# Two attention layers on one core: the weighted values in two blocks of four key tiles a half, instead of three blocks of three, two and three

## What is computed

```
xn  = group_norm(x, 32 groups) * gamma + beta
qkv = w_qkv @ xn + b_qkv                      # 8 heads of 32 channels
m   = softmax((q * s)^T (k * s))              # 1024 x 1024 for each head
a   = m v
x   = x + w_proj @ a + b_proj
```

## Time and profile before

| | us |
|---|---|
| three executions | 2036.97, 2041.02, 2039.26 (median 2039.26) |
| the profiled execution: its own time | 2038.87 |
| its span, first to last instruction | 2037.1 |
| PE busy | 2015.1 (99%) |
| DVE, ACT, POOL busy | 1676.5 (82%), 1242.8 (61%), 1836.8 (90%) |
| mean granted TensorE clock | 0.997 of full speed |

### The profile page before, as it was taken

How to read it: one execution, slowest core, us unless ns; L and a number is a source line. 1 busy time by engine, 2 the same in 40 slices (tenths; PEclk the granted TensorE clock), 3 DMA queues, 4 the chain that set the end, 5 groups by cost and what they waited for, 6 DMA issues and landing times.

```text
span 2037.1 us, 30395 instructions
## 1 busy us (share of the span) xinstructions
PE 2015.1 (99%) x10134; PEld 1141.0 (56%) x10134; DVE 1676.5 (82%) x2871; ACT 1242.8 (61%) x2321; POOL 1836.8 (90%) x626
## 2 busy tenths in 40 slices
PE   8999999999999999999999999999999999999998
PEld 5565555655556565555555556555565655555543
DVE  5888888888888888888888888888888888888881
ACT  2656656666665666656566566666656566565664
POOL 2799999999999999999999999999999999999984
PEclk9999999999999999999999999999999999999999
DMA  4455445644536545456554456445465454554521
GB/s 131 84 109 119 95 110 110 144 100 94 120 84 145 117 102 110 92 122 145 112 112 100 110 113 139 106 89 119 89 146 113 103 112 91 123 125 87 116 48 42
DMA packets 217307, 220.31 MB, mean 108 GB/s; under 512 B 167489, under 2 KB 167617, under 8 KB 209345
## 3 DMA queue, kind: packets, MB, share of 16 engines
q1 hardware_dynamic: 208032, 153.50, 33.6%
q0 software_dynamic: 8784, 63.97, 15.7%
q10 hardware_dynamic: 336, 0.92, 0.2%
HBM read 36.32 MB, written 16.78 MB: 26 GB/s over the span
## 4 chain that ended last, share of the span: by engine, by line
PE 94%; DVE 3%; ACT 3%; DMA 0%; issue 0%; SPq 0%; POOL 0%; DVEq 0%; ACTq 0%; POOLq 0%
PE ps_s L434 24%; PE ps_v L488 22%; PE ps_s L464 21%; PE ps_d L519 10%; PE ps_d L534 5%; PE ps_d L527 5%; PE ps_s L510 4%; ACT pt L743 2%; DVE raw_max L827 1%; ACT stage_kh L762 1%; DVE neg_max L848 1%; PE ps_s L644 0%; PE ps_s L519 0%; DMA par<-pars_dram 0%; PE ps_s L659 0%
## 5 line engine op out<-in xcount | busy, mean ns | idle before, releaser
L743 ACT ACTIVATE pt<-ps_s 128x512 f32<-128x512 f32 x2048 | 1116.7, 601 | 739.8 <-PE ps_s L434 733.1
L827 DVE TENSOR_REDUCE raw_max<-ps_s 128x1 f32<-128x512 f32 x2008 | 1289.7, 684 | 259.0 <-PE ps_s L464 254.8
L1015 POOL TENSOR_TENSOR acc<-acc,pt 128x2048 f32<-128x2048 f32 x315 | 1441.2, 4575 | 44.6 <-ACT pt L743 1.3
L464 PE MATMUL ps_s<-ks,qs 96*128 96x512 f32 x2008 | 968.6, 482 | 1.8 <-DVE neg_max L848 1.0
L434 PE MATMUL ps_s<-qs,ks 97*128 97x512 f32 x2048 | 837.2, 410 | 4.6 <-ACT pt L743 1.2
L434 PEld LDWEIGHTS ps_s<-qs,ks 97*128 97x128 f32 x2048 | 388.8, 190 | 324.8 <-issue 187.9
L464 PEld LDWEIGHTS ps_s<-ks,qs 96*128 96x128 f32 x2008 | 380.0, 189 | 182.7 <-DVE raw_max L827 75.1
L488 PE MATMUL ps_v<-pt,v 128*32 128x512 f32 x4096 | 478.7, 596 | 0.0
L1015 POOL TENSOR_TENSOR acc<-pt 128x2048 f32<-128x2048 f32 x64 | 299.6, 4681 | 58.7 <-ACT pt L743 57.1
L488 PEld LDWEIGHTS ps_v<-pt,v 128*32 128x32 f32 x4096 | 120.0, 110 | 272.6 <-issue 217.5
L519 PE MATMUL ps_d<-xn,wq 128*128 128x512 f32 x492 | 253.6, 596 | 0.0
(11 more groups left out here) (61 smaller groups left out, 601.9 us busy)
## 6 DMA issues: line engine op xcount, KB each, us to landing
acc<-pt POOLq DMA_DIRECT2D x61, 1024.0 KB, 8.5
qs<-stage_qh SPq DMA_DIRECT2D x256, 128.0 KB, 2.4
ks<-stage_kh SPq DMA_DIRECT2D x251, 128.0 KB, 2.4
qs<-stage_ql SPq DMA_DIRECT2D x128, 128.0 KB, 2.5
qs<-neg_max SPq DMA_DIRECT2D x1024, 0.5 KB, 2.1
ks<-stage_kl SPq DMA_DIRECT2D x126, 128.0 KB, 2.4
xn<-x_dram SPq DMA_DIRECT2D x16, 512.0 KB, 4.5
res<-x_dram SPq DMA_DIRECT2D x16, 512.0 KB, 4.3
```

What stands on the lines that cost most here:

```text
L464: pe.matmul(ps_m[place % RING][:, :], qs[b][0:KROWS, h, c:c + P], ks[b][0:KROWS, h, kf * HALF:(kf + 1) * HALF], start=True, stop=True).the ...
L743: act.activation(tile_of(half, t)[:, h, :], ps_t[(UNITS * s.n + u) % RING][:, :], ACT.Exp, scale=SCALE).then_inc(exp_done, 1)
L827: dve.tensor_reduce(raw_max[:, e % 2, t, kf:kf + 1], ps_m[MAX_PLACE["max", UNITS * n + w] % RING][:, :], AX.X, ALU.max)\
L1015: pool.tensor_tensor(acc[hf][:, :, :], a[:, :, :], tile_of(half, t)[:, :, :], ALU.add).then_inc(pool_added, 1)
```

## The change

The lists of units are replaced; no function changes. The order of PE's instructions changes, and with it that of the few instructions of ACT and DVE that follow a unit.

```diff
-PV_BLOCKS = {2: (-3, -2, -1), 12: (0, 1), 22: (2, 3, 4)}
-LAST_TILES = 3
-VALUES_OUT_AT = 3
-DENSE_AT = ((5, 10), (16, 20), (25, 26), (30, 33), (37, 40), (47, 51), (56, 58), (63, 64))
-SUMS_AT = 22
-SUMS_AT_END = 12
+PV_BLOCKS = {4: (-4, -3, -2, -1), 20: (0, 1, 2, 3)}
+LAST_TILES = 4
+VALUES_OUT_AT = 5
+DENSE_AT = ((7, 10), (14, 18), (23, 26), (30, 33), (40, 42), (47, 49), (54, 57), (62, 64))
+SUMS_AT = 20
+SUMS_AT_END = 4
 ROWS_AT = 7
 START_PARTS = (0, 2, 1, 3)
 V_AT, QK_AT = (1, 3, 5, 7), (1, 3)
 V_OUT_AFTER, LOW_AFTER = (3, 5), (7, 11, 15, 19)
 BUSY = 3, 12
-STATS_AT = (36, 43, 52, 53)
-GN_AT = 6
+STATS_AT = (35, 37, 51, 52)
+GN_AT = 7
```

## The result

The changed kernel takes **2048.0 us** (median of six runs, 2043.4 to 2050.1); the kernel before took 2038.0 us beside it. The ratio is 1.0048 (95% interval 1.0038 to 1.0058): slower by 10 us. The profiled execution took 2048.54 us, 9.7 more than the one of before, and its span is 2046.7.

What follows compares the result with a forecast made beforehand. PE, busy 99% of the span, was taken as the bound. Eight pairs +10.7, six pairs -1.0, four other slots -1.6, start +1 and end +2.5 gave +11.6 on 2038.87: 2050.5 us, range 2023 to 2058.

Steps and rivals of the forecast that it cites:

- the wait for half A's DMA: PE waits at unit 52's sums for POOL's accumulating DMA: 2.4 us in eight pairs, 0.7 in six.
- The runs of four: Four units without dense work, beginning with ACT's copy of q or k; a second per slot costs 0.26 us more.
- DVE and the rest of the stretches: DVE keeps up over 15 to 16 units between blocks: costed at nothing, otherwise 0.1 to 0.3 us a half.
- Fewer blocks: Four blocks a slot on PE instead of six, 0.33 us each: 1.32 us less a pair, about 21 over 32 slots.
- rival 4: Block cost grows with its tiles, so nothing is saved: near 2060 us; chance 0.02.
- Statistics later, sums earlier: Group statistics, then half A's adds and DMA, come 1.33 us later, its sums 2.46 earlier: margin shrinks by 3.79 us.
- Rival 1: The DMA's landing doesn't hold half A's sums: 2028.7 us, without the extra runs 2020.4; chance 0.24.
- rival 2: The landing holds half A's sums, but takes 7.5 us everywhere: 2038.5 us; chance 0.18.
- that rule's sum: With 2.0 us fixed DMA cost, layer 0 lands 1.3 us earlier, layer 1 0.7 later: total some 6 us lower.
- rival 3: DVE or ACT stalls PE late between longer blocks, 0.1 to 0.3 us a half: 2056 to 2064; chance 0.06.
- Half B, start: Half B's sums wait 0.2 us a pair in layer 1, 0 in layer 0; slots 0 and 1 add 1 us.
- The end: Second last half's sums move from unit 44 to 36, where PE waits for POOL's adds: +2.5 us (1 to 6).

Runs made afterwards that it cites:

- experiment 5: Changed kernel with four blocks of two tiles a half instead of two of four, two tiles left at the end: 2068.7 us.
- experiment 3: Changed kernel with POOL's scale and shift behind half A's first add and ACT's normalising instructions at units 21, 25, 29, 33: 2040.4 us.
- experiment 9: Kernel before with ACT's copy of q or k put ahead of the exponential of the same unit: 2031.3 us.
- experiment 8: Kernel before with its dense step at (37, 40) moved to (36, 38), making a run of six units without dense work: 2071.8 us.
- experiments 1 and 2: Dense steps respaced: changed kernel, (40, 42) to (39, 43) and (54, 57) to (54, 58), 2073.8 us; kernel before, (56, 58) to (56, 59), 2053.2 us.
- experiment 6: Changed kernel with only SUMS_AT_END put back from 4 to 12: 2048.9 us.

## Why the prediction was right, and where it was not

The direction and the total (2050.5 against 2048.0) came out, and each step of the path is in the trace: the statistics, the issue, the landing, the sums that wait for it. The division of the loss did not. The forecast gave the wait for half A's DMA 8 x 2.4 + 6 x 0.7 = 23 us and said that most of the gain turns into it; it was about 5, of the 31 us that stand against the gain of 21. The runs of four, put at 5 us, took 13 to 14, and DVE and the rest of the stretches, put at nothing, took 6. That these errors nearly cancel is luck: with the wait as it came and the rest as forecast, the sum would have been about 2032.

- **Fewer blocks: right.** A block of four tiles takes 3.57 us, and the score matmul behind it 0.43. 0.33 a block holds for two, three and four tiles (experiment 5), so rival 4 falls. The Trainium skill, page TensorEngine Tiling (Array Packing), section Key Properties, says "Changing tiling mode (not just tile) drains the TensorE". The trace agrees: the column tiled matmuls of line 488 pay 0.33 us once a block and nothing more per tile; that this time is the drain, no run separates.
- **Statistics later, sums earlier: right as a path.** The statistics came 10.75 us behind unit 0 against 10.5 to 10.7, the issue 31.1 to 31.4 behind that; and all 14 sums of half A begin 0.13 to 0.14 us behind the landing, where before they had 0.9 to 3.2 us to spare. Rival 1, that the landing doesn't hold the sums, falls. One size was off: PE was ready for these sums 1.7 to 1.85 us earlier in the pair than before, not 2.46, since the new run of four lies ahead of them (0.4) and the stretches there are longer (0.3).
- **The size of that wait: wrong in layer 0.** The step was "*Between landings of 7.5 and 9.7 us I take each layer's own*". Layer 0's landings took 7.4 to 8.3 us in the changed kernel, not 8.8 to 9.7, and layer 1's 7.4 to 7.6 as before. So the wait was 0.57 us in the mean of the eight pairs and 0.33 in that of the six, 0.44 and 0.20 without the 0.13 of every start, where I had 2.4 and 0.7. That was rival 2's condition, that the landings shorten, and it got a chance of 0.18. Its time of 2038.5 didn't come, because the runs and the rest cost more. A pair in layer 0 took 124.3 us, not 125. The DMA traffic in 40 slices of 0.25 us from 215 us, around layer 0's first landing, is to be laid beside the earlier trace rows:

```profile
GB/s 0 33 2 0 0 2 0 2 1 524 0 426 98 0 524 0 328 197 0 525 0 361 164 0 525 0 262 262 0 3 1 0 68 0 0 2 0 0 0 0
```

  The bulk starts at 217.25, 1.5 us behind the issue at 215.76, and ends at 222.0; the landing, 7.8 us behind the issue, is at 223.6. So traffic takes about as long as before (4.75 us), and it is the tail behind it that fell from 3.3 to 1.6 us. In layer 1 it is 1.2 (before: 1.3). The Trainium skill, page DMA: Bandwidth & Descriptors, section Anatomy of one DMA - SWDGE (gpsimd) path, has a nearly constant 2.0 us of fixed cost; the trace doesn't agree with a constant, but that rule's sum, some 6 us lower, erred by less than my rows did in this term. Why the tail shortened stays open. It isn't the later issue: in experiment 3 the issue is at 40.5 us of the pair as before, and layer 0 still lands at 7.5 to 8.8. It goes with the kernel's lists of units, blocks or dense steps: with those of before and another order on ACT (experiment 9) layer 0 still lands at 8.8 to 9.6.
- **Runs of four: too small.** I took 0.26 us a run from one interval of the earlier trace rows. The whole stretch, start to start, costs 0.40: 0.28 lies ahead of that unit's scores, as in the earlier trace rows, and the rest in the dense step behind it, 0.10 at its first matmul and 0.07 at its second. Also the working "*in a pair's first slot it only shortens that wait*" made one of two new runs free, and with a wait of only 0.5 us little of it was. 32 runs at 0.40 cost 13 us; I had 14 x 0.26 and four more, 4.7. This term made up for nearly half of what the wait was too long by.
- **DVE at nothing: too small.** The stretches' rest grew by 0.4 us a pair, 6 us in all. The bound of 0.1 to 0.3 a half holds it, the value of nothing doesn't; that all of it is DVE's isn't shown. That a longer run makes DVE the bound (0.91 us for a matmul in experiment 8) is the mechanism of rival 3, in a place where the change hadn't put it; and that the four-tile block covers the divide, as the prediction says, is borne out by experiment 5, where two tiles don't. The prediction's sentence that results are out in time when the next step comes "*at least four units after the last*" is wrong for q and k (experiments 1 and 2); in the changed kernel these steps have five.
- **Half B, start: right in size.** Half B's sums are held by tenths of a microsecond in some pairs; the start moved by 1.0 us.
- **The end: right in size, for another reason.** I had +2.5; the profiled executions show +3.7 from the last pair on. 1.7 of it lies behind the last unit, where four tiles are left instead of three; the prediction has no term for that. The wait of 2.13 us for POOL is there, but putting the sums back to where they were gained nothing, since a wait for DVE takes its place (experiment 6).

## What to carry to other kernels

Fewer, larger blocks save their switching cost, but each block moved also moves a deadline and breaks or joins a run of the other work. Before such an edit, list for each producer with a small margin (here 1 us) by how much its own start and its user move, and then the longest stretch without filler work; and where a wait appears, look for an engine that was idle just before the late instruction. Changing the order of two instructions there (POOL's statistics behind its first add, ACT's copy ahead of the exponential) was worth 7 to 8 and 10 us, and the second was worth 5 to 8 in the kernel before too. So try the new order on the old arrangement as well, before the gain is put down to the arrangement.

A forecast whose total comes true isn't yet right: compare its terms one by one. Here the largest was four to five times too large.

Price such a wait by a whole stretch from start to start and not by its one widest interval: the two differed by half here.

## What the runs showed that I had not expected

- The same 1 MB accumulating DMA, issued at the same point of POOL's order (half A), lands after 7.4 to 9.7 us in the two kernels; in the one place where I compared the traffic, the difference lies behind the last of its bulk.
- A step of q or k holds its PSUM bank for more than four units (about 1.9 us at 0.47 each) behind its last matmul: with four units the next step starts 0.8 to 0.9 us late, with five about 0.1.
- Without dense matmuls, the cost of a run depends on what ends it and grows faster than its length: nothing for four units with a block behind them, 0.4 us for four with a dense step behind them, and about 1.2 for six (1.35 less the 0.18 of that stretch before).
